# Attention layer on one core: linear pieces cut into quarters and placed by a table of half slots

## The reference

```
x = x + proj(attention(layernorm(x)))      # rotary q and k, ALiBi bias, softmax over 512 keys
x = x + ffn(layernorm(x))                  # ffn(x) = x W' + b + (x V_r) C'
attention: q, k, v = layernorm(x) @ qkv_w.T ; q, k rotated by position
           softmax(q k' / 4 + min(key - query, 0) * slope[head] * 8) @ v
```

## Time and profile before

| | us |
|---|---|
| median of 3 runs | 2185.89 |
| lowest, highest | 2172.15, 2186.41 |
| profiled execution | 2183.17 |
| its span in the trace | 2181.5 |

### The profile page before, as it was taken

The page is one execution under the profiler, slowest core; times in us unless marked ns, Lnnn a source line. Parts: engine busy times, 40 slices in busy tenths (PEclk is TensorE's granted clock), DMA queues, the critical chain, the costliest instruction groups (busy, mean ns, idle before and its releaser), DMA issues.

```text
span 2181.5 us, 77783 instructions
## 1 busy us (share of the span) xinstructions
PE 2113.5 (97%) x31524; PEld 1121.9 (51%) x31524; DVE 1890.0 (87%) x5439; ACT 1530.0 (70%) x2562; POOL 1299.9 (60%) x1095
## 2 busy tenths in 40 slices
PE   5999999999999999999999999999999999999996
PEld 2345555555555555555555555555555555555553
DVE  5689889888989998988988998999898898899962
ACT  2267777777777777777777777777777777777662
POOL 6366666656565666666666656566666666665511
PEclk8699999999999999999999999999999999999997
DMA  5233333333333333333333333333333433333310
GB/s 162 77 96 90 105 118 93 105 117 98 93 109 93 110 109 101 98 103 119 92 106 115 99 92 110 94 109 109 103 97 103 120 91 105 116 98 93 100 33 25
DMA packets 158871, 218.50 MB, mean 100 GB/s; under 512 B 19025, under 2 KB 104913, under 8 KB 158513
## 3 DMA queue, kind: packets, MB, share of 16 engines
q1 hardware_dynamic: 157232, 211.44, 32.6%
q10 hardware_dynamic: 1280, 2.10, 0.3%
HBM read 36.52 MB, written 16.78 MB: 24 GB/s over the span
## 4 chain that ended last, share of the span: by engine, by line
PE 89%; DVE 6%; issue 3%; ACT 1%; POOL 1%; SPq 0%; DVEq 0%; DMA 0%; POOLq 0%; ACTq 0%
PE ps_s L390 28%; PE ps_o L411 20%; PE ps_misc L374 17%; PE ps_misc L361 12%; PE ps_misc L352 3%; PE ps_t L398 3%; DVE junk L561 3%; PE ps_misc L430 3%; PE ps_misc L421 2%; DVE attn_t L587 1%; DVE ps_t L571 0%; ACT o_sb L804 0%; ACT pt L715 0%; DVE row_max L561 0%; POOL x_hat L826 0%
## 5 line engine op out<-in xcount | busy, mean ns | idle before, releaser
L561 DVE CUSTOM_DVE_ANT_0 junk<-ps_s,alibi 128x512 bf16<-128x512 f32 x2048 | 1330.7, 687 | 227.9 <-PE ps_s L390 198.7
L715 ACT ACTIVATE pt<-ps_t 128x1024 f32<-128x1024 f32 x1024 | 1048.5, 1024 | 464.0 <-DVE ps_t L571 449.1
L390 PE MATMUL ps_s<-at 64*128 64x512 f32 x2048 | 803.7, 460 | 25.4 <-DVE row_max L561 12.1
L398 PE MATMUL ps_t<-at 64*128 64x512 f32 x2048 | 761.1, 449 | 2.1 <-ACT pt L715 1.9
L411 PE MATMUL ps_o<-pt,v_one 128*17 128x128 f32 x16384 | 640.6, 274 | 4.0 <-ACT pt L715 1.4
L411 PEld LDWEIGHTS ps_o<-pt,v_one 128*17 128x17 f32 x16384 | 429.4, 98 | 311.7 <-issue 211.3
L571 DVE SCALAR_TENSOR_TENSOR ps_t<-diag,slope,ps_t 128x256 f32<-128x256 f32 x1024 | 488.8, 477 | 19.1 <-PE ps_t L398 19.1
L390 PEld LDWEIGHTS ps_s<-at 64*128 64x128 f32 x2048 | 323.0, 187 | 281.7 <-DVE row_max L561 240.4
L887 POOL TENSOR_TENSOR rope_b<-raw,rope_sin 128x512 f32<-128x512 f32 x128 | 164.9, 1288 | 368.1 <-ACT raw L776 368.0
L908 POOL TENSOR_TENSOR halves<-rope_a,swapped 128x512 fp32r<-128x512 f32 x128 | 161.8, 1285 | 357.9 <-DMA swapped<-rope_b 357.9
L398 PEld LDWEIGHTS ps_t<-at 64*128 64x128 f32 x2048 | 315.4, 185 | 34.5 <-ACT pt L715 26.2
(11 more groups left out here) (91 smaller groups left out, 1603.2 us busy)
## 6 DMA issues: line engine op xcount, KB each, us to landing
at<-halves SPq DMA_DIRECT2D x192, 512.0 KB, 3.7
swapped<-rope_b SPq DMA_DIRECT2D x256, 128.0 KB, 2.6
x_in<-in_L_attn_x_dram SPq DMA_DIRECT2D x32, 512.0 KB, 5.2
num<-o_sb SPq DMA_DIRECT2D x512, 32.0 KB, 2.0
x_res<-in_L_attn_x_dram SPq DMA_DIRECT2D x32, 512.0 KB, 5.4
out_dram<-x_hat SPq DMA_DIRECT2D x32, 512.0 KB, 6.0
at<-spread_den SPq DMA_DIRECT2D x60, 64.0 KB
at<-max_t ACTq DMA_DIRECT2D x128, 16.0 KB
```

The source lines that it names most:

```text
L390: pe.matmul(ps_s[:, t % 2, :], operand(n, 0)[:, t * P:(t + 1) * P], operand(n, 1), start=True, stop=True).then_inc(s_done, 1)
L398: pe.matmul(ps_t[:, j, :], operand(n, 1)[:, j * P:(j + 1) * P], operand(n, 0), start=True, stop=True).then_inc(t_done, 1)
L561: dve.tensor_tensor_reduce(junk[:, t % 2, :], ps_s[:, t % 2, :], alibi[:, off:off + N], 1.0, LOWEST, ALU.add, ALU.max, row_max[:, hb % 2, ...
L715: act.activation(pt[:, h % 2, 2 * pair:2 * pair + 2, :], ps_t[:, 2 * pair:2 * pair + 2, :], ACT.Exp).then_inc(exp_done, 1)
```

## The change

```
-QK_BEGIN = (-12, -11, -5, -2)
-XT_BEGIN = -13
...
+        def due(half, begin, counts=(1,)):
+            for i, count in enumerate(counts):
+                b, off = divmod(half - begin - i, 2 * H)
+                if off == 0 and 0 <= b < NB:
+                    return b, range(sum(counts[:i]), sum(counts[:i]) + count)
+            return None, ()
...
+        def complete_at(half, begin, counts=(1,)):
+            b, off = divmod(half - begin - len(counts) + 1, 2 * H)
+            return b if off == 0 and 0 <= b < NB else None
...
-            def project_qk(cc, kc, bank):
+            def project_qk(cc, quarter, bank):
+                part, kc = divmod(quarter, KC)
+                columns = slice(part * C, (part + 1) * C)
...
-                    ins = pe.matmul(bank[q * QUARTER:(q + 1) * QUARTER, :], wqkv_t[:, kc, col:col + QUARTER],
-                                    xt[:, kc, :], start=(kc == 0), stop=(kc == KC - 1), skip_group_check=True)
+                    ins = pe.matmul(bank[q * QUARTER:(q + 1) * QUARTER, columns], wqkv_t[:, kc, col:col + QUARTER],
+                                    xt[:, kc, columns], start=(kc == 0), stop=(kc == KC - 1), skip_group_check=True)
...
-                if slot == QK_BEGIN[1] + 1:
+                if slot == -8:
                     finish_weights()
...
+                    for c in range(4):
+                        b, quarters = due(now, *QK[c])
+                        for quarter in quarters:
+                            if quarter == 0:
+                                bank = misc_bank("qk")
+                            project_qk(4 * b + c, quarter, bank)
...
+            def empty_bank(now):
+                slot, half = divmod(now, 2)
...
+                cc = chunk_complete(now)
+                if cc is not None:
+                    act.wait_ge(misc_full, full_at["qk", cc])
+                    if cc:
+                        act.wait_ge(rope_done, cc)
+                    act.copy(raw[:, :], ps_misc[:, :]).then_inc(raw_done, 1)
...
+                empty_bank(2 * slot)
                 b = sooner_at(slot, -19)
...
-                    take_squares(b, 2)
                     take_squares(b, 3)
...
+                empty_bank(2 * slot + 1)
...
                 if b:
                     take_mean(b, 3)
+                    take_squares(b, 2)
...
-                cc = chunk_at(slot, 1)
+                cc = chunk_rotated(slot)
```

More of the change, by code:

```diff
@@ L308, in half_at, with chunk_complete, chunk_rotated @@
             return hb if off == 0 and 0 <= hb < 2 * NB else None
-        def chunk_at(slot, after):
-            for c, begin in enumerate(QK_BEGIN):
-                b = batch_at(slot, begin + after)
+        def due(half, begin, counts=(1,)):
[7 more added lines that the diff above has]
+            return b if off == 0 and 0 <= b < NB else None
+        def chunk_complete(half):
+            for c, piece in enumerate(QK):
+                b = complete_at(half, *piece)
+                if b is not None:
+                    return 4 * b + c
+            return None
+        def chunk_rotated(slot):
+            for c, begin in enumerate(ROTATE):
+                b = batch_at(slot, begin)
                 if b is not None:
@@ L353, in turn_tokens @@
                 misc_filled(ins, (kind, b, kc), done, KC * b + kc + 1)
-            def project_qk(cc, kc, bank):
+            def project_qk(cc, quarter, bank):
                 b, f, s = chunk_of(cc)
-                if kc == 0 and cc % 4 == 0:
+                part, kc = divmod(quarter, KC)
+                if quarter == 0 and cc % 4 == 0:
                     pe.wait_ge(xt_done, KC * (b + 1))
+                columns = slice(part * C, (part + 1) * C)
                 for q in range(QUARTERS):
@@ L364, in project_qk, with linear @@
+                if quarter == 3:
                     misc_filled(ins, ("qk", cc), raw_done, cc + 1)
-            def linear(half, bank, kind, b, u, src, weight, ready, ready_count, done):
-                if u == 0 and half == 0:
+            def linear(quarter, bank, kind, b, u, src, weight, ready, ready_count, done):
+                if u == 0 and quarter == 0:
                     pe.wait_ge(ready, ready_count)
[L370 to L377, removed]
+                part, kc = divmod(quarter, KC)
+                t = 2 * u + part
+                for q in range(QUARTERS):
+                    tok = t * P + q * QUARTER
+                    ins = pe.matmul(bank[q * QUARTER:(q + 1) * QUARTER, part * C:(part + 1) * C],
+                                    src[:, kc, tok:tok + QUARTER], weight[:, kc, :],
+                                    start=(kc == 0), stop=(kc == KC - 1), skip_group_check=True)
+                if quarter == 3:
@@ L467, in tensor_program @@
                 n, nt, nv = head_at(slot, 0), head_at(slot, T_LAG), head_at(slot, PV_LAG)
[L468 to L480, removed]
+                hb = half_at(slot, 8)
+                if slot == -12:
                     pe.wait_ge(qkv_scaled, 1)
-                if slot == QK_BEGIN[1] + 1:
+                if slot == -8:
                     finish_weights()
@@ L487, in tensor_program @@
                 for half in range(2):
+                    now = 2 * slot + half
                     for t in (2 * half, 2 * half + 1):
@@ L492, in tensor_program @@
                             exp_scores(nt, t)
[L493 to L503, removed]
@@ L504, in tensor_program @@
-                    b = batch_at(slot, 39)
-                    if b is not None:
-                        turn_tokens("x2t", b, half, x_hat2, xhat_done2, b + 1, x2t_done)
+                    for u in range(2):
+                        b, quarters = due(now, *V[u])
+                        for quarter in quarters:
+                            if quarter == 0:
+                                bank = misc_bank("v", b, u)
+                            linear(quarter, bank, "v", b, u, xt, wqkv_t[:, :, 2 * C:3 * C], xt_done, KC * (b + 1),
+                                   v_staged)
+                        b, quarters = due(now, *PROJ[u])
+                        for quarter in quarters:
+                            if quarter == 0:
+                                bank = misc_bank("proj", b, u)
+                            linear(quarter, bank, "proj", b, u, attn_t, proj_t, attn_done, KC * (b + 1), x1_done)
+                        b, quarters = due(now, *FFN[u])
+                        for quarter in quarters:
+                            if quarter == 0:
+                                bank = misc_bank("ffn", b, u)
+                            linear(quarter, bank, "ffn", b, u, x2t, ffn_t, x2t_done, KC * (b + 1), y_done)
@@ new lines, in tensor_program @@
+                    for c in range(4):
+                        b, quarters = due(now, *QK[c])
+                        for quarter in quarters:
+                            if quarter == 0:
+                                bank = misc_bank("qk")
+                            project_qk(4 * b + c, quarter, bank)
+                    for kc in range(KC):
+                        b, quarters = due(now, XT[kc])
+                        if b is not None:
+                            turn_tokens("xt", b, kc, x_hat, xhat_done, b + 1, xt_done)
+                        b, quarters = due(now, X2T[kc])
+                        if b is not None:
+                            turn_tokens("x2t", b, kc, x_hat2, xhat_done2, b + 1, x2t_done)
+                        b, quarters = due(now, DEN[kc])
+                        if b is not None:
+                            spread_denominators(b, kc)
@@ L646, in vector_program @@
                             denominators(b, part)
-                    b = batch_at(slot, 31)
-                    if b is not None:
-                        divide(b, half)
+                    now = 2 * slot + half
+                    for kc in range(KC):
+                        b = complete_at(now, DEN[kc])
+                        if b is not None:
+                            divide(b, kc)
                     for u in range(2):
-                        b = batch_at(slot, 33 + u)
-                        if b is not None and half == 1:
+                        b = complete_at(now, *PROJ[u])
+                        if b is not None:
                             add_linear("proj", b, u, x1, x_res, res_biased, x1_done)
-                        b = batch_at(slot, 41 + u)
-                        if b is not None and half == 1:
+                        b = complete_at(now, *FFN[u])
+                        if b is not None:
                             add_linear("ffn", b, u, y, y, x1_biased, y_done)
@@ L663, in scalar_program, with copy_turned @@
             act = nc.scalar
-            def copy_turned(kind, b, kc, dst, scale, done):
+            def copy_turned(kind, b, kc, dst, done):
                 act.wait_ge(misc_full, full_at[kind, b, kc])
```

(29 more changed lines are left out.)

11 lines of the change are left out of this document (removed).

## The result

| | before | changed |
|---|---|---|
| median, us | 2179.02 (4 runs) | 2228.38 (4 runs) |
| lowest, highest | 2172.13, 2186.41 | 2223.80, 2237.89 |
| profiled execution: span | 2181.5 | 2227.2 |

The changed kernel takes 1.0232 times as long (95% interval 1.0174 to 1.0289).

A forecast was written before the change was run, and what follows sets the result against it. TensorE was taken to bound full halves, a loop through TensorE, VectorE and ScalarE the bare ones. Loss 43 minus gain 13 gave +30 on 2183.17, so 2213, with 2.7 for the median 2216 us; range 2166 to 2240.

The forecast's parts named there:

- Halves 29 to 1: Batch end into the next (32 halves a batch): 10.12 to 11.55 us, TensorE awaiting split maxima; 43 us loss.
- rival 2: Raw's copy of piece 3 up to 0.8 us sooner, stall halved: 2184 to 2195; chance 0.15 together with (4).
- One sign: In half 1, the turnings of the maxima would start within 0.1 us of the end of GpSimd's split.
- Halves 9 to 17: Middle of a batch: 16.90 to 16.46 us, x_hat2's turning waiting 0.75; gain taken as 0.4 each, 13.4 us in all.
- Quarter halves: Halves with one quarter of a q and k piece: 1.73 us each, 1.65 where the engine loop has slack.
- the loop: TensorE's exponent scores, VectorE's maxima and diagonal, ScalarE's exponential, then that pair's next scores: 3.47 us a slot, 1.73 a half.
- At least 3.47 us, however little TensorE does: Claimed minimum time of any slot, set by the loop; VectorE's own sum put at 1.70 us a half.
- The rest: Divides, transfers, moved squares, unchanged halves, start and end: no price; 256-column cutting of q and k also counted as nothing.
- Start and end: 0, within 2 us: Before the first and behind the last batch: no change, within 2 us either way.
- (1): GpSimd doesn't hold the maxima: halves 29 to 1 take 9.9 us, 9 to 17 take 16.0; 2153 us; chance 0.15.
- (3): Each of 8 quarter halves costs 0.1 us more, both chains keep their stalls: 2241 us; chance 0.1.
- (4): The spread does nothing: GpSimd's order repays each batch TensorE's gain, 2180 to 2190 us; chance 0.15 together with rival 2.

The follow-up runs named there:

- piece 3 alone late: Changed kernel with the table of the kernel before, except piece 3 spread to halves 28, 29, 30 and denominator spreads in 31 and 0: 2254.08 us, ratio 1.0331.
- the one-number edit: Changed kernel with GpSimd rotating piece 3 in slot 0 instead of slot 15, behind the splitting of the maxima: 2154.97 us, ratio 0.9887 against the kernel before.
- the old table: Changed kernel with its table set to the halves of the kernel before, keeping 256-column quarters, copy order and moved squares: 2183.06 us, ratio 0.9998.
- piece 3 back: Changed kernel with piece 3 of q and k back in halves 28 and 29, denominator spreads staying in 31 and 0: 2176.61 us, ratio 0.9979.

## Why the prediction was right, and where it was off

The measured change is +49 us by the medians and +45.6 by the spans; forecast was +30. The time, 2228.38, lies 12 us above the 2216 forecast. By its own steps:

- *Halves 29 to 1.* Forecast 11.55 us, with TensorE waiting 2.0 for the split; measured 11.57 and 2.00. Raw's copy was put at 3.4 to 4.0 and lay at 3.38 to 3.96; GpSimd's row at 6.30 and was 6.29. Over the run +42.3 against +43. Shown by the run with piece 3 alone late, and by the one-number edit that takes the cause away. The chain of rows had it right because it followed the order on ScalarE and GpSimd. ScalarE's order is the smaller part of the shift: TensorE itself had the last quarter done only at 1029.47 (3.08 us into half 29), so without the exponential ahead of it the copy could have come some 0.2 us sooner (an estimate: before, it began 0.07 us behind TensorE's last matmul), and not the 0.8 of rival 2. One sign was missed: the turnings start 0.15 us behind GpSimd, not within 0.1.
- *Halves 9 to 17.* Forecast 16.5, measured 16.55, over the run -11.8 against -13. Quarter halves take 1.67 to 1.78, 3.46 for two: the loop (3.47) and not TensorE's own 1.65, as said; in halves 11 to 14 each pair's exponent scores start 0.05 us behind the exponential that they wait for. Half 9 shows the parts: 0.67 us to the quarter, 0.45 for it, 0.55 behind it, against 0.66, 0.44 and 0.55, so no price of a change of mode is to be seen. x_hat2's turning waited 0.75 in the batch shown, 0.72 as a mean of 29 (20.9 us). That it is the forecast to the hundredth is luck: TensorE came to the turning and started it each some 0.15 us later than forecast.
- *"At least 3.47 us, however little TensorE does"* is not so. In batch 31 of the kernel before, slots without a piece take 3.19 and 3.21 us (halves that start at 2053.64, 2056.83 and 2060.04), with VectorE busy throughout at 1.61 us a half, not 1.70: the next row maximum starts 0.39 us behind a diagonal. The loop takes 3.47 where VectorE has to wait for the scores first, as in halves 12 to 14 of before and 11 to 14 of the changed kernel, so the sum isn't touched.
- *The rest.* The cutting into quarters, put at nothing, is nothing (ratio 0.9998). The squares that moved, put at nothing too, cost 4 us in half 11 with the old table and none in the new one, where raw's copy no longer stands in half 9 beside them. "Start and end: 0, within 2 us" was wrong by a few: -6.0, of which -4.5 behind the start of the last half. There the granted clock stands at half of full speed for 32.0 us in the kernel before and 21.6 in the changed one. The same work in the last output projection takes 3.64 us before, at a clock of 0.50, and 1.93 us in the run with the old table, at 1.00. Over all ten kernels this end takes 75 us with 17 us at the low clock, 77 to 83 with 22 to 32, and 86 to 90 with 42: it goes with the clock. Why the clock falls there for longer in one kernel than in another stays open. (The kernel before has its clock low at the end as well, not only at the start.)
- *What was off* is a term that the sum didn't have. I held TensorE's clock at 1.00 since a whole batch showed it, and then forecast that TensorE would stand idle 2.0 us in every batch without asking what that does to the clock. In 12 of the inner batches it fell to half in half 2: up to 3.70 instead of 2.10, +18.8 us over the run. (Batch 1, with a wait of 2.75 us, fell too.) The forecast batch of 65.4 to 65.7 us is there only without a fall; the others take some 67.1. By the spans the terms are 42.3 - 11.8 + 18.8 + 2.3 - 6.0 = 45.6. That 30 + 19 also makes the 49 of the medians is chance, and so is that the time missed by 12 us only: the shorter ends and the 2.7 us added for the median worked against the missing 19. The rows of before couldn't price it in half 2, but the stretches ahead of the first slot and behind the last, where the clock is low in the page's PEclk line, should have been asked.
- *The rivals.* None came about. GpSimd does hold the maxima (1), the copy wasn't sooner (2), quarter halves didn't cost 0.1 more (3), and GpSimd's order cost more than TensorE won, 42.3 against 11.8 us, instead of repaying it (4).

## What to carry to other kernels

Before moving a producer later, list what its consumer's engine has queued behind that consumer: here a step of 2.5 us that nobody was in a hurry for stood ahead of a chain of 3.8 us that TensorE needed, and a shift of 1.6 us in its input came out as a stall of 2.0 on another engine. If a table schedules one engine, the order on the others belongs in the same table: moving the rotation behind the steps that are waited for turned +2.3% into -2.0%. And price a stall of TensorE with the clock that follows it, not only with its length.

## What the runs showed of the hardware

- A pause of 2.00 us in TensorE's work (1.98 to 2.01 us in 29 batches of the changed kernel) was followed by a fall of the granted clock from 1.00 to half, 2.4 to 1.2 GHz, in 12 of them and by none in the other 17, with the pause and the work around it the same. What picks the 12 stays open. In the kernel with piece 3 alone late it was 19 of 29. With the pause filled by other matmuls (14 or 32 calls) it was none, and without a pause (piece 3 back, or rotated behind the split) none either. The Trainium skill ("TensorE: Matmul & The Clock Gate", "What's actually happening") says that the throttled state is the default and that activity releases it; these runs agree, in that the same wait costs no clock once TensorE is active in it.
- A fall cost up to 1.6 us in the full half that it met (3.70 against 2.10), so that a pause of 2.0 us cost 3.6 where one followed.
- The end of the kernel, with the same work in it, took 74.8 to 90.4 us, roughly longer the longer the granted clock was at half: 17.1 us of it in the shortest, 42.1 in the longest (42.4 in another of 86.4). The sums over the halves of inner batches leave this out.
